# Layer 0's query-major mask: turned from the key-major mask on TensorE instead of loaded from DRAM

## The reference

```python
x = x + _L0_xattn_ref(ctx_1024, ctx_1024, _layernorm(x), mask, ...)
x = x + _L0_attn_ref(_layernorm(x), ...)
x = x + _L0_ffn_ref(_layernorm(x), ...)
x = x + _L1_xattn_ref(_layernorm(x), ctx_1024, ctx_1024, ...)
x = x + _L1_attn_ref(_layernorm(x), ...)
x = x + _L1_ffn_ref(_layernorm(x), ...)
```

```python
energy = jnp.einsum('nqhd,nkhd->nhqk', q, k)
energy = jnp.where(mask == 0, jnp.float32(-1e+20), energy)
attention = jax.nn.softmax(energy / jnp.sqrt(jnp.float32(EMBED)), axis=3)
out = jnp.einsum('nhql,nlhd->nqhd', attention, v).reshape(n, q_len, EMBED)
return out @ Wo.T + bo
```

## Time and profile before

| | us |
|---|---|
| median of 3 runs | 4396.85 (4392.42 to 4407.57) |
| the profiled execution, by its own time | 4394.22 |
| its span in the trace | 4392.5 |
| start of layer 0's `cross_attention` in the trace | 397.6 |
| first matmul of its maxima | 408.2 |
| end of the last masked maximum of head 0 | 477.9 |
| first score matmul | 483.7 |
| layer 1, which has no mask: start of its `cross_attention` | 2538.5 |
| layer 1: first matmul of the maxima, end of the last maximum of head 0 | 2544.5, 2586.7 |
| fill of the two extra rows of the key ring by POOL in layer 0 | 397.8 to 409.6 |

### The profile page before, as it was taken

The page is one execution under the profiler, slowest core; times in us unless marked ns, Lnnn a source line. Parts: engine busy times, 40 slices in busy tenths (PEclk is TensorE's granted clock), DMA queues, the critical chain, the costliest instruction groups (busy, mean ns, idle before and its releaser), DMA issues. The chain is left out here.

```text
span 4392.5 us, 50969 instructions
## 1 busy us (share of the span) xinstructions
PE 3877.4 (88%) x17656; PEld 2209.3 (50%) x17656; DVE 2997.9 (68%) x3608; ACT 2355.4 (54%) x3611; POOL 1695.3 (39%) x1007
## 2 busy tenths in 40 slices
PE   7996899999999685668999779999999979769997
PEld 6884344444444261137788534444444425347885
DVE  4333877878787359954888667777777734477886
ACT  2221477777777533312777426666566641247775
POOL 0001487787778606510000126666556650000000
PEclk9997899999999878889999869999999999779998
DMA  9997566676666400021888646666666550407886
GB/s 317 329 339 263 168 155 156 154 155 149 154 152 145 120 5 10 0 80 41 331 323 325 239 127 154 154 144 152 139 153 151 122 132 1 107 31 295 323 327 242
DMA packets 301737, 753.52 MB, mean 172 GB/s; under 512 B 55854, under 2 KB 89390, under 8 KB 267946
## 3 DMA queue, kind: packets, MB, share of 16 engines
q1 hardware_dynamic: 245322, 562.03, 38.7%
q0 software_dynamic: 47456, 171.46, 19.5%
q10 hardware_dynamic: 8704, 16.78, 1.1%
HBM read 485.01 MB, written 99.42 MB: 133 GB/s over the span
## 5 line engine op out<-in xcount | busy, mean ns | idle before, releaser
L776 ACT ACTIVATE prob<-psum 128x512 f32<-128x512 f32 x1552 | 891.4, 595 | 437.1 <-PE psum L676 399.0
L951 POOL TENSOR_TENSOR den_pool<-den_pool,prob 128x1024 f32<-128x1024 f32 x372 | 938.8, 2524 | 228.6 <-DVE den_pool L863 196.8
L676 PE MATMUL psum<-q_stack,k_ring 98*128 98x512 f32 x2048 | 1006.1, 509 | 20.4 <-ACT prob L776 14.5
L651 PE MATMUL psum<-k_ring,q_stack 96*128 96x512 f32 x2048 | 693.1, 423 | 106.1 <-DVE row_max L834 36.4
L830 DVE TENSOR_REDUCE row_max<-psum 128x1 f32<-128x1024 f32 x512 | 616.0, 1220 | 243.7 <-PE psum L651 240.6
L834 DVE CUSTOM_DVE_ANT_0 psum<-psum,mask_q 128x1024 f32<-128x1024 f32 x512 | 627.1, 1233 | 202.9 <-PE psum L651 187.8
L676 PEld LDWEIGHTS psum<-q_stack,k_ring 98*128 98x128 f32 x2048 | 395.3, 194 | 621.8 <-ACT prob L776 272.4
L1928 DVE TENSOR_TENSOR weight_lo<-weight_raw,weight_hi 128x2048 fp32r<-128x2048 f32 x240 | 548.0, 2289 | 132.6 <-ACT weight_hi L1871 131.5
L694 PE MATMUL psum<-prob,x 128*32 128x512 f32 x3104 | 517.5, 613 | 0.9 <-ACT prob L776 0.9
L651 PEld LDWEIGHTS psum<-k_ring,q_stack 96*128 96x128 f32 x2048 | 395.2, 200 | 213.5 <-issue 84.5
L1871 ACT ACTIVATE weight_hi<-weight_raw 128x2048 fp32r<-128x2048 f32 x240 | 457.7, 1917 | 69.9 <-DMA weight_raw<-in_L_ffn_w 35.5
(11 more groups left out here) (428 smaller groups left out, 6351.0 us busy)
## 6 DMA issues: line engine op xcount, KB each, us to landing
weight_raw<-in_L_ffn_w SPq DMA_DIRECT2D x120, 1024.0 KB, 6.9
den_dma<-prob POOLq DMA_DIRECT2D x204, 512.0 KB, 5.0
k_ring<-k_hi SPq DMA_DIRECT2D x1024, 64.0 KB, 2.3
weight_raw<-in_L_ffn_Wu SPq DMA_DIRECT2D x60, 1024.0 KB, 7.2
weight_raw<-in_L_ffn_Wd SPq DMA_DIRECT2D x60, 1024.0 KB, 5.8
den_dma<-xnT POOLq DMA_DIRECT2D x68, 512.0 KB, 4.9
k_ring<-k_lo SPq DMA_DIRECT2D x512, 64.0 KB, 2.6
ctxT<-in_ctxT SPq DMA_DIRECT2D x16, 1024.0 KB, 9.6
```

The lines of the kernel that those rows point to most:

```text
L651: ins = e.matmul(max_banks(q)[:, a * KC:(a + 1) * KC], q_stack[h % n_q][0:QROWS, i * P:(i + 1) * P], k_ring[0:QROWS, (n + a) % kring, :], ...
L676: e.matmul(k.bank(b % 2), k_ring[:, n % kring, kt * P:(kt + 1) * P], q_stack[h % n_q][:], start=not masked, stop=True, skip_group_check=ma ...
L776: e.activation(prob[b // 2 % n_p][:, b % 2, :], k.bank(b % 2), ACT.Exp, scale=scale).then_inc(s_exp, 1)
L951: e.tensor_tensor(den[:], den[:], tile, ALU.add).then_inc(s_dpool, 1)
```

## The change

The 32 mask DMAs on ACT's queue and the 32 conversions on DVE are gone. `turn_mask(q)` on TensorE takes eight blocks of 128 keys by 128 queries of mask_k as stationary operand and `ident_big` as moving operand, eight matmuls of 128 columns, into two banks: 0 and 1 for even q, 6 and 7 for odd. These banks are otherwise first used by the scores (0, 1), the value sums (6) and the small matmuls (7), all later. ACT copies the 1024 columns from PSUM into mask_q (one instruction for each q, 32 in all). TensorE may write the turned banks of q once ACT has copied q-2, and DVE's pair q waits for ACT's copy q. The first score matmul also waits for all 32 copies, and the wait of the exponentials for the mask buffers goes.

```diff
+            def turn_mask(q):
+                c2, i = divmod(q, TT)
+                if q >= 2:
+                    e.wait_ge(s_maskq, q - 1)
+                for t in range(2 * KC // P):
+                    out = k.bank(turned_banks(q)[t // (KC // P)])
+                    ins = e.matmul(out[:, t % (KC // P) * P:(t % (KC // P) + 1) * P],
+                                   masks[1][:, 2 * c2 * (KC // P) + t, i * P:(i + 1) * P], k.ident_big[:],
+                                   start=True, stop=True)
+                ins.then_inc(s_maskT, 1)
...
+                    if masked:
+                        e.wait_ge(s_maskq, PAIRS)
...
+            if masked:
+                turn_mask(0)
+                turn_mask(1)
             for q in range(PAIRS + LEAD):
                 if q == PAIRS + 1:
                     max_rows(0)
                 maxima(q)
+                if masked and q + 2 < PAIRS:
+                    turn_mask(q + 2)
...
             if masked:
-                for n in range(2 * NKC):
-                    c, j = divmod(n, 2)
-                    if n >= n_p:
-                        e.wait_ge(s_maskq, n - n_p + 1)
-                    e.dma_start(prob[n % n_p].bitcast(I32), mask_rows[:, 2 * j:2 * j + 2, chunk_cols(c)]
-                                ).then_inc(s_mq[n % n_p], 16)
+                for q in range(PAIRS):
+                    c2, i = divmod(q, TT)
+                    a = turned_banks(q)[0]
+                    e.wait_ge(s_maskT, q + 1)
+                    e.activation(masks[0][:, i, 2 * c2 * KC:2 * (c2 + 1) * KC],
+                                 k.psum[:, a:a + 2, :].rearrange("p b n -> p (b n)"), ACT.Copy).then_inc(s_maskq, 1)
...
-                if h == 0 and i % 2 == 0:
-                    e.wait_ge(s_maskq, 4 * c2 + 2 + i // 2 + 1)
+                if h == 0:
+                    e.wait_ge(s_maskq, q + 1)
...
-                if masked and q < PAIRS and q % TT == 0:
-                    for n in range(q, q + 4):
-                        c, j = divmod(n, 2)
-                        e.wait_ge(s_mq[n % n_p], 16 * (n // n_p + 1))
-                        e.tensor_scalar(masks[0][:, 2 * j:2 * j + 2, chunk_cols(c)], prob[n % n_p].bitcast(I32), 0,
-                                        NEG_BIG, ALU.is_equal, ALU.mult).then_inc(s_maskq, 1)
```

More of the change, by code:

```diff
@@ L567, in cross_attention @@
     s_wo, s_xback = k.sem("s_wo"), k.sem("s_x_back")
-    s_mq = [k.sem("s_mask_q") for _ in range(n_p)]
     s_sign, s_ring = k.sem("s_lo_sign"), k.sem("s_ring_init")
@@ L577, in cross_attention @@
     s_osb, s_head, s_att, s_rec = k.sem("s_o_sb"), k.sem("s_head_out"), k.sem("s_att"), k.sem("s_den_rec")
-    s_maskq, s_proj, s_xadd = k.sem("s_mask_q_done"), k.sem("s_proj"), k.sem("s_x_added")
+    s_maskT, s_maskq = k.sem("s_mask_turned"), k.sem("s_mask_q_done")
+    s_proj, s_xadd = k.sem("s_proj"), k.sem("s_x_added")
     vbank, misc = k.bank(6), k.bank(7)
@@ L588, in max_banks, with turned_banks @@
         return k.psum[:, 2 + 2 * (q % 2):4 + 2 * (q % 2), :].rearrange("p b n -> p (b n)")
+    def turned_banks(q):
+        return (0, 1) if q % 2 == 0 else (6, 7)
     with nc.Block() as block:
@@ L750, in _ @@
         def _(e):
-            mask_rows = k.i["mask"].rearrange("(i p) k -> p i k", p=P)
             def m_hi_rows(h):
@@ L759, in tile_free @@
                 if g < n_p:
-                    if masked:
-                        e.wait_ge(s_maskq, 2 * NKC)
                     return
```

## The result

The changed kernel takes 4366.61 us in the median of 5 runs (4358.88 to 4372.59), against 4396.85 before: a ratio of 0.9932 with a 95% interval of 0.9913 to 0.9952, or 30.2 us less. The forecast was 4365, a gain of 32. The profiled execution took 4371.98 us, 22.2 less than that of before, with a span of 4370.3.

The account below looks back on a forecast made before the run. DVE, fed partly by mask DMAs, was taken to bound head 0's maxima. 404.9 + 1.7 + 32 x 1.20 = 445.0 instead of 477.9 saves 32.9 us, 32 in total: 4396.85 to 4365, range 4357 to 4384.

Parts of the forecast that it names:

- The bound: Head 0's maxima, 400 to 478 us: DVE bounds, fed by mask DMAs first, then only by its own work.
- What goes: Head 0's maxima: 19.3 us of DVE conversions, 13.6 us of mask waits, and the mask's competition with the keys.
- The front: Start of layer 0's block: without mask loads the first maxima matmul comes at 403.6, 6.0 us after the start as in layer 1.
- ACT's copy: One copy of 1024 columns per pair on otherwise idle ACT: 1.04 us, hidden unless a pair takes less.
- The small matmul: TensorE's eight 128-column matmuls per pair: 0.08 us each at full clock (1.11 a pair), 0.15 at half (2.06).
- The clock: TensorE in head 0's maxima: about 4 us at half clock from 403.6, costing 1.7 us, then full.
- The chain: Last maximum to first score, 5.8 us: loses about 1 us, as turned maxima take 1.86 us at half clock.
- The sum: Head 0's last maximum ends at 445.0 instead of 477.9, 32.9 us earlier; total gain 32 us, handovers maybe 2 us.
- Dear small matmuls: Rival in head 0's maxima: 0.11 us each, TensorE bounds at 1.35 us a pair, gain 28.1, time 4370; chance 0.10.
- serial weight loads: Rival on TensorE: weight loads not fetched ahead, 4.5 us a pair at half clock, time 4468, a loss; chance 0.03.
- the half clock: Rival: TensorE stays at half clock through head 0's maxima, 1.72 to 2.38 us a pair, 4378 to 4400; chance 0.12.
- ACT or a PSUM conflict slowing DVE: Rival in head 0's maxima: smaller gain; ACT's copy would have to exceed 2.28 us to undo it; no separate chance given.

Follow-up runs that it names:

- e_seven_dmas: Kernel before with only the first 7 of 32 mask DMAs, DVE still making all 32 conversions; 4389.34 us, ratio 0.9983.
- e_turn_7dmas: Changed kernel plus seven unneeded mask DMAs on ACT's queue at the block's start; 4378.76 us, ratio 0.9949 to the kernel before.
- e_copy_x2: Changed kernel with ACT copying each turned mask twice; 4390.10 us, ratio 0.9976 to the kernel before.
- e_turn_x3: Changed kernel with each turn matmul issued three times, 24 instead of 8 per pair; 4382.77 us, ratio 0.9961 to the kernel before.
- e_act_convert_7: Kernel before with only 7 mask DMAs and ACT making all 32 conversions, no turning; 4381.72 us, ratio 0.9962.
- e_dve_copy: Changed kernel with DVE instead of ACT copying the turned mask from PSUM; 4410.31 us, ratio 1.0028 to the kernel before.
- a_again: The changed kernel measured again, unaltered; 4363.22 us, ratio 0.9926 to the kernel before.
- b_warm: Changed kernel plus extra matmuls nobody reads, before the first maximum and around the end of head 0's maxima; 4362.34 us, ratio 0.9916 to the kernel before.
- e_act_convert: Kernel before with all 32 mask DMAs kept but ACT making the conversions instead of DVE; 4393.43 us, ratio 0.9988.

## Why the prediction was right

Point by point, in its order.

- **The bound.** DVE bounds the stretch, fed by loads in its first half and by its own work in the second: this holds, and e_seven_dmas shows the second half bare (7.34 us a group). Under "What goes" the forecast priced the conversions at 19.3, "all on the path", and the waits at 13.6; its total came from the other side, as a new start and 32 paces. The waits behind the first are 15.0, as the 13.6 left out one for a load into xnT. Neither price holds for its cause alone: the conversions moved to ACT bring 6.7, most of the loads gone 9.4, both together 21.8.
- **The front.** Forecast: the first maxima matmul 6.0 us after the block's start, from layer 1's row. Measured 5.7, and e_turn_7dmas gives the 5.2 us back to the loads.
- **ACT's copy.** Forecast 1.04, measured 1.02, and 0.98 back to back. It hides, as forecast; e_copy_x2 shows 1.96 us a pair as the price when it doesn't.
- **The small matmul.** Forecast 0.08 at full clock (0.057 to 0.11) and 0.15 at half (0.107 to 0.19), measured 0.055 and 0.105, just outside the lower ends. This is the term that was off by most. It did no harm, as DVE is the slower at 1.18 either way; in e_turn_x3, with TensorE as the bound, it would have. The reason given, that the load of two-byte weights takes half of the float32's time, pointed the right way and should have been followed further. The Trainium skill's 81 ns ("TensorE: Matmul & The Clock Gate", "Back-to-back issue gap") does not hold for this form: at 0.055 a pair takes 0.99 and not 1.12.
- **The clock.** Forecast: about 4 us at half clock, then full. Measured 4.5, from 404.82 to 409.33, at a cost of 410.67 - 406.16 - 3 x 1.18 = 1.0 us to DVE where 1.7 was forecast. Reasoning from layer 1 (gaps keep it at half) and from the kernel's start (dense work raises it) was borne out by pairs of kernels: beside the same seven loads the clock is full from 418 to 440 us with the turning (e_turn_7dmas) and 0.50 without it (e_act_convert_7), and it is 0.50 in e_dve_copy, which has the turning and gaps. The Trainium skill's rule for transpose mode ("TensorE: Matmul & The Clock Gate", "Part 4: PE-mode transpose") does not reach these plain matmuls with an identity: the clock is 1.00 beside them from 410 to 440 us.
- **DVE's pace.** Forecast 1.20, measured 1.18 with no wait. 32 times 0.02 is 0.6 us.
- **The chain.** Forecast to lose 1 us, measured a gain of 0.3 (0.5 in a_again). The reason given for the loss was none: the 1.86 us at half clock are of the kernel before, so they are in its 5.8 already. After the change the turned maxima ran at full clock, in 1.03 us. What the forecast didn't see is that the clock falls back just behind them (446.53, four matmuls in 1.98), which b_warm prices at part of 1.9 us.
- **The sum.** 32.9 for the last maximum, less 1 for the chain, makes the 32 of the forecast; the 2 us for handovers were named there and not taken off. The trace shows nothing to take off: from the first maximum's start to the last's, DVE takes 31 x 1.18 us and the 1.0 of the clock. Measured by the same steps it is 34.4 for the last maximum and 0.3 for the chain. The 2.8 us more are 1.3 in the chain and 1.5 elsewhere: some 0.3 in the front, 0.6 in DVE's pace and 0.7 in the cheaper pairs at half clock. By the first score the forecast was thus low by these 2.8; that its 32 lies between the gains of the two medians, 30.2 and 35.6 for the same code, confirms it less closely than it seems. The lower bound holds a slip: 477.9 - 442.3 is 35.6 and not 36.6, and moves 4357 to 4358.
- **Hidden work.** The queries of head 1 came in time: its first maxima matmul, at 444.1, waits only for DVE. POOL's fill ends at 409.5, and no matmul behind it waits for a load of values.
- **The rivals.** Dear small matmuls are ruled out by 0.055, serial weight loads by 0.105 at half clock, the half clock by the windows. ACT or a PSUM conflict slowing DVE is ruled out by 1.18 us beside an ACT that is busy 87% of the time from 430 to 440 us.
- **The test that was set wrongly.** The forecast said that it would be wrong as a whole if anything behind 484 us changed by more than 3. In the one pair of traces layer 1's mixer changed by 5.8, and all behind the first score by 11. The same code run again has it at 38.7: 3 us was less than the stages' own spread from run to run, which the forecast had no second trace to learn from.

## What to carry to other kernels

When an engine waits for loads in one half of a stretch and works through in the other, the two causes cover each other: ask what is left when only one goes, and add their prices only for a change that removes both. Work moved to an idle engine is free only up to the pace of the bound; here the same copy costs nothing on ACT at 1.02 us and 41 us on DVE. Judge an early, local change by a landmark right behind it, counted from the start of its block, and by medians; the span of one trace carried 23 us of chance from elsewhere.

## What the runs showed of the hardware

- Added work can make TensorE faster. Maxima with no turning beside them ran at 1.2 GHz and 1.32 us each for as long as they lasted (e_act_convert_7); with eight small matmuls more per pair the clock went to 2.4 GHz and they ran at DVE's 1.18 (the changed kernel and, beside the same seven loads, e_turn_7dmas).
- With waits between bursts the clock went up and down: in e_copy_x2, where TensorE waits for ACT in most pairs, stretches of 10 us read 0.93 and 0.66 with the same instructions. It fell after the turned row maxima in the changed kernel and stayed up in b_warm.
- The same stage of the same code had the clock at 0.61 over its last 15 us in one run and 0.80 in another (layer 1's mixer, after and a_again), and lasted 43.6 and 38.7 us. I have no cause for it.
- With keys and mask loading together the DMA engines moved 305 to 328 GB/s at a share of 1.05 to 1.08 (e_turn_7dmas, 402 to 418 us), and a piece of mask of 512 KB arrived every 2.9 us (e_act_convert).
- ACT's copies of 1024 columns from PSUM are 0.98 us apart in a row and 1.02 alone, even where every second one waits for a semaphore that the one before it set (e_copy_x2).
